# All norms of a fused two-layer transformer block: the variance and factor of a chunk taken in turn with the centering and square of the next

## The reference

```python
def _layernorm(x, axis=-1, eps=1e-05):
    m = jnp.mean(x, axis=axis, keepdims=True)
    v = jnp.var(x, axis=axis, keepdims=True)
    return (x - m) / jnp.sqrt(v + eps)

def rmsnorm(x, w):
    return x * jax.lax.rsqrt(jnp.mean(x * x, axis=-1, keepdims=True) + EPS) * w
...
x = L0_attn_a_x
x = x + _L0_attn_a_ref(_layernorm(x, axis=-1), ...)
x = x + _L0_ffn_ref(_layernorm(x, axis=-1), ...)
x = x + _L0_attn_b_ref(_layernorm(x, axis=-1), ...)
x = x + _L0_ffn_ref(_layernorm(x, axis=-1), ...)
x = x + _L1_attn_a_ref(_layernorm(x, axis=-1), ...)
x = x + _L1_ffn_ref(_layernorm(x, axis=-1), ...)
x = x + _L1_attn_b_ref(_layernorm(x, axis=-1), ...)
x = x + _L1_ffn_ref(_layernorm(x, axis=-1), ...)
```

## Time and profile before

| | |
|---|---|
| median of 3 runs | 1047.9 us (1047.13 to 1048.45) |
| profiled execution | 1043.13 us, span 1041.0 us |
| mean granted TensorE clock | 0.945 |
| PE busy | 949.4 us (91%) |
| ACT busy | 541.9 us (52%) |
| DVE busy | 535.3 us (51%) |
| POOL busy | 146.2 us (14%) |

### The profile page before, as it was taken

One profiled execution on the slowest core, in us unless ns is written; L12 is line 12 of the kernel. 1 busy time (PEld: TensorE's weight loads), 2 busy tenths in 40 slices (PEclk: granted clock), 3 DMA queues, 4 the chain that ended last, 5 costly groups with the idle time before them and its releaser, 6 DMA issues.

```text
span 1041.0 us, 23939 instructions
## 1 busy us (share of the span) xinstructions
PE 949.4 (91%) x10552; PEld 442.3 (42%) x10552; DVE 535.3 (51%) x870; ACT 541.9 (52%) x767; POOL 146.2 (14%) x164
## 2 busy tenths in 40 slices
PE   7489969899999988997899799997999999999998
PEld 4257743423333335883333334433333333344443
DVE  4356725733333266665465445546666666423554
ACT  6024445689999946443655551246454454445121
POOL 4101020331001003110011040000233223004000
PEclk9789999999999998559999899999999999998999
DMA  7653140010000000000000036400000000001651
GB/s 205 202 150 101 53 169 0 0 42 2 2 2 2 2 1 2 4 4 1 1 0 0 1 76 150 104 1 0 2 3 2 2 2 2 0 1 29 160 130 51
DMA packets 16479, 43.23 MB, mean 42 GB/s; under 512 B 4812, under 2 KB 5260, under 8 KB 14700
## 3 DMA queue, kind: packets, MB, share of 16 engines
q1 hardware_dynamic: 16376, 41.71, 14.7%
HBM read 36.91 MB, written 4.55 MB: 40 GB/s over the span
## 4 chain that ended last, share of the span: by engine, by line
PE 78%; ACT 8%; DVE 6%; issue 2%; DMA 2%; SPq 2%; POOL 1%; DVEq 0%; POOLq 0%
PE ps L1599 77%; ACT nrr L816 2%; ACT nrr L814 1%; DMA stf<-aux 1%; ACT work L1059 1%; POOL work L665 1%; SPq L578 1%; ACT work L860 0%; DVE mxq L1220 0%; DVE work L1553 0%; ACT nrr L803 0%; ACT nrr L800 0%; DVE stf L1567 0%; SPq L572 0%; DMA stf<-scr_k 0%
## 5 line engine op out<-in xcount | busy, mean ns | idle before, releaser
L1599 PE MATMUL ps<-rq,stf 32*64 32x512 f32 (+4 forms) x4096 | 213.5, 469 | 3.5 <-ACT hz L964 1.6
L1599 PE MATMUL ps<-work,vbuf 64*32 64x96 f32 (+6 forms) x3712 | 197.2, 386 | 2.4 <-issue 2.2
L1599 PE MATMUL ps<-hz,wsb 128*128 128x512 f32 (+1 forms) x352 | 159.3, 608 | 6.3 <-ACT nsq L805 3.5
L1599 PEld LDWEIGHTS ps<-rq,stf 32*64 32x64 f32 x4096 | 102.1, 152 | 108.4 <-issue 85.8
L920 ACT ACTIVATE work<-ps 128x1024 f32<-128x1024 f32 x144 | 139.4, 1022 | 13.4 <-PE ps L1599 10.0
L1599 PEld LDWEIGHTS ps<-work,vbuf 64*32 64x32 f32 (+1 forms) x3712 | 72.5, 121 | 112.6 <-issue 65.2
L982 ACT ACTIVATE work<-ps 128x1024 f32<-128x1024 f32 x72 | 73.6, 1024 | 75.7 <-PE ps L1599 75.7
L1599 PEld LDWEIGHTS ps<-hz,wsb 128*128 128x128 f32 (+1 forms) x352 | 61.7, 188 | 86.2 <-issue 67.5
L1301 DVE TENSOR_TENSOR work<-work,csb 128x1024 f32<-128x1024 f32 (+1 forms) x40 | 41.6, 1040 | 95.8 <-ACT work L920 95.4
L1028 ACT ACTIVATE work<-ps 128x512 f32<-128x512 f32 x48 | 28.7, 597 | 117.2 <-PE ps L1599 117.2
L1599 PE MATMUL ps<-work,wsb 128*128 128x512 f32 (+1 forms) x176 | 86.9, 602 | 2.7 <-DVE work L1514 2.7
(11 more groups left out here) (194 smaller groups left out, 1163.4 us busy)
## 6 DMA issues: line engine op xcount, KB each, us to landing
stf<-scr_w SPq DMA_DIRECT2D x32, 256.0 KB, 4.5
stf<-scr_w SPq DMA_DIRECT2D x64, 128.0 KB, 3.4
stf<-scr_k SPq DMA_DIRECT2D x12, 204.0 KB
stf<-scr_q SPq DMA_DIRECT2D x12, 192.0 KB
wsb<-in_w SPq DMA_DIRECT2D x1, 2192.0 KB, 11.0
rq<-in_rq SPq DMA_DIRECT2D x2, 1024.0 KB, 8.2
scr_q<-work SPq DMA_DIRECT2D x6, 256.0 KB, 5.1
scr_k<-work SPq DMA_DIRECT2D x6, 256.0 KB, 5.6
```

What stands on the lines that cost most here:

```text
L1599: return nc.tensor.matmul(o, l, r, start=start, stop=stop, skip_group_check=True)
```

## The change

TensorE takes center c + 1 ahead of mean c, and ScalarE square c + 1 ahead of factor c; before, each did one kind for all four chunks first. In the twins ScalarE runs two squares first. No instruction is added or dropped, and VectorE, GpSimd and SyncE keep their order.

```diff
             def norm(n):
                 src, _, kind, _, _, _ = nrm(n)
-                for c in range(NC):
+                e = eps[:, 0:1] if kind == "ln" else eps[:, 1:2]
+
+                def square(c):
                     if kind == "ln":
                         act.wait_ge(n_cen, centered_up_to(n, c))
                         nc.scalar.activation(nsq[:, c], bank(c), ACT.Square).then_inc(n_sq, 1)
...
+                def factor(c):
                     act.wait_ge(n_var, squared_up_to(n, c))
                     nc.scalar.activation(nrr[:, c], bank(4 + c), ACT.Ln, bias=e).then_inc(n_ln, 1)
-                    act.wait_ge(n_ln, i + 1)
+                    act.wait_ge(n_ln, 4 * n + c + 1)
                     nc.scalar.activation(nrr[:, c], nrr[:, c], ACT.Exp, scale=-0.5).then_inc(n_r, 1)
...
+                square(0)
+                if n not in TWINS:
+                    for c in range(1, NC):
+                        square(c)
+                        factor(c - 1)
+                    factor(NC - 1)
+                    return
+                square(1)
+                for c0 in range(0, NC, 2):
+                    for c in (c0, c0 + 1):
+                        twin_factor(c)
+                        if c + 2 < NC:
+                            square(c + 2)
+                    for c in (c0, c0 + 1):
+                        nc.scalar.activation(nsq[:, c], bank(4 + c), ACT.Ln, bias=eps[:, 0:1]).then_inc(n_ln, 1)
+                    if n != 2:
+                        for c in (c0, c0 + 1):
+                            hidden_factor(n, c)
...
             def norm(n):
                 src, _, kind, _, _, _ = nrm(n)
-                if kind == "ln":
-                    for c in range(NC):
+                for c in range(NC + 1):
+                    if c < NC and kind == "ln":
                         wait_source(pe, n, c)
                         mm(bank(c), c_("center"), ch(src, c)).then_inc(n_cen, 1)
-                for c in range(NC):
-                    pe.wait_ge(n_sq, squared_up_to(n, c))
-                    mm(bank(4 + c), c_("mean"), nsq[:, c]).then_inc(n_var, 1)
+                    if c:
+                        pe.wait_ge(n_sq, squared_up_to(n, c - 1))
+                        mm(bank(3 + c), c_("mean"), nsq[:, c - 1]).then_inc(n_var, 1)
```

More of the change, by code:

```diff
@@ L794, in norm @@
                         nc.scalar.activation(nsq[:, c], ch(src, c), ACT.Square).then_inc(n_sq, 1)
[L795 to L809, removed]
@@ L810, in norm, with twin_factor @@
-                e = eps[:, 0:1] if kind == "ln" else eps[:, 1:2]
-                for c in range(NC):
-                    i = 4 * n + c
+                def factor(c):
                     act.wait_ge(n_var, squared_up_to(n, c))
                     nc.scalar.activation(nrr[:, c], bank(4 + c), ACT.Ln, bias=e).then_inc(n_ln, 1)
-                    act.wait_ge(n_ln, i + 1)
+                    act.wait_ge(n_ln, 4 * n + c + 1)
                     nc.scalar.activation(nrr[:, c], nrr[:, c], ACT.Exp, scale=-0.5).then_inc(n_r, 1)
+                def twin_factor(c):
+                    _, e2, at = TWINS[n]
+                    act.wait_ge(n_var, squared_up_to(n, c))
+                    nc.scalar.activation(nrr[:, c], bank(4 + c), ACT.Ln, scale=1.0 + e2,
+                                         bias=eps[:, at:at + 1]).then_inc(n_ln, 1)
+                    act.wait_ge(n_ln, second(n, c))
+                    nc.scalar.activation(nrr[:, c], nrr[:, c], ACT.Exp, scale=-0.5).then_inc(n_r, 1)
```

## The result

The changed kernel took 1041.53 us in the median of 11 executions (1036.67 to 1048.25), the kernel before 1048.45 in 11 on the same chip (1041.99 to 1055.95): a ratio of 0.9941, 95% interval 0.9913 to 0.9968, or -6.2 us. The ratios are taken over the fast executions alone, the means that stand beside some of them over all, and the two ways differ by up to 2 us.

The account below looks back on a forecast made before the run. TensorE was taken to hold 78% of the chain of waits, ScalarE 8%. Norm by norm, -0.94 - 1.30 + 0.74 + 0.43 + 0.10 - 0.15 - 0.64 = -1.76 us, from 1047.9 to 1046.1 us, range 1043.2 to 1048.6.

Parts of the forecast that it names:

- The size of one norm: In a centered norm: first factor 1.7 us earlier, last factor 0.65 earlier, last variance matmul on TensorE ends 0.43 later.
- Norms 1 and 2: Norm 1, before a linear layer, gains 0.47 us; norm 2, a twin before VectorE's rotary product, gains 0.65.
- Norms 5 and 6: Norm 5, before a linear layer, gains 0.47 us; norm 6, before the location layer, where TensorE sets the pace, loses 0.43.
- Norm 4: No centering there; squares 2 and 3 now stand behind Exps, so last Exp and rotary product come later: loss 0.74 us.
- Norm 7: Before the router's gates, four groups of about 1 us that end about where they end now: gain 0.05 us.
- Norm 8: A twin, with VectorE as the chain to the residual that releases norm 10's centering: gain 0.65 us.
- Norm 12: Before the router's gates, four groups of about 1 us that end about where they end now: gain 0.10 us.
- all norms wait for the last factor: Rival: TensorE's queue never matters, so all eleven norms gain 0.65, 7.2 us together: 1040.8 us; chance 0.06.
- the low stretch behind norm 12 goes: Rival: the new order closes small gaps between the router's gates, ending the low clock, 2.9 us: 1043.2 us; chance 0.18.
- the fall behind norm 4: Rival: TensorE's new waits in norm 4 lower the clock through 15 us behind it, 7.5 us more: 1053.6; chance 0.07.
- table switches: Rival: squares between factors make ScalarE reload its activation tables in each norm: over 1100 us; chance 0.01.
- I carry the difference: Last step: median before lies 4.8 us above the profiled execution; this is kept, so 1047.9 - 1.8 = 1046.1 us.

Follow-up runs that it names:

- whole2: The changed kernel again, unaltered, on another chip, against the kernel before: ratio 0.9973 (0.9944 to 1.0001), -2.8 us.
- all_but_12: The changed kernel with the old order in norm 12 only, against the kernel before: ratio 1.0002 (0.9976 to 1.0028).
- null: The old order in every norm, written in the changed kernel's code (same program as before), against the kernel before: ratio 0.9981 (0.9951 to 1.0011).
- only_12: The kernel before with the new order in norm 12 only, against the kernel before: ratio 1.0006 (0.9978 to 1.0034).

## Why the prediction was wrong, and where it was right

The three comparisons of the changed kernel with the one before give -6.9, -1.8 and -1.8 us in the means (standard errors 1.7, 1.0 and 1.3), together -2.7 with 0.7. By the ratios they are -6.2, -2.8 and -0.2, together -3.3 with 0.9. The forecast of the change, -1.8, fits the second and third and the joint value; the first lies 2.4 of its errors from the mean of the three. What made that one -6.9 stays open: the clocks of its executions of the kernel before were not kept. No norm or group of norms gave by its total more than its step; the stage behind norm 12 did in the profiles.

- *The size of one norm.* The mechanism holds in every centered norm that was read: first factor earlier (-1.62, forecast -1.7), last factor -0.55 (forecast -0.65), TensorE's last mean later, +0.58 (forecast +0.43). The term that was missing is the 0.10 of a mean that waits for its square and has its weights loaded only then; it shifts all three the wrong way.
- *Norms 1 and 2:* -0.55 to z 3 and -0.50 from there, -1.05 in all; forecast -0.47 - 0.65 = -1.12.
- *Norms 5 and 6:* center to last z -0.56 or more (with the low clock at its start, 483 us, 9.43 before and 8.68 in whole3), then +0.72 to norm 6's last copy, the sum about +0.1; forecast -0.04.
- *Norm 4:* +0.74, as forecast, in every profile with the new order on both engines and full clock there (all_but_12 had a low stretch at 381, and 8.00 for 7.08).
- *Norm 7:* z 3 comes 0.5 to 0.6 earlier, and from there to the first routed share it takes 25.88 for 25.63 at full clock and 27.57 for 27.33 with a low stretch of 3.4 us: -0.3 in all; forecast -0.05.
- *Norm 8:* from the last residual ahead of it to its z 3 10.94 for 11.58, -0.64; forecast -0.65. *Norm 10:* +0.15; forecast +0.10. *Norm 11:* -0.56; forecast -0.64.
- *Norm 12:* z 3 -0.55, and 0.2 to 0.3 of it is left at the routed shares when profiles with an equal low stretch are compared; forecast -0.10. But in all three profiles of the changed kernel the low stretch was 3.4 us, and in both of the kernel before (before and null) 6.8, so the whole stage took 35.62 to 35.68 for 37.24 and 37.56: some 1.6 to 1.9 less. TensorE behind norm 12, before and then after:

```profile
936.54 3.19 PE L1599 MATMUL ps<-wsb,hz 128*128 128x16 f32 x16 [0.17 <-DVE hz L1122]
939.66 12.78 PE L1599 MATMUL ps<-hz,wsb 128*64 128x512 f32 x32
```

```profile
934.06 3.96 PE L1612 MATMUL ps<-wsb,hz 128*128 128x16 f32 x32
937.95 12.04 PE L1612 MATMUL ps<-hz,wsb 128*64 128x512 f32 x32
```

- *Norm 0:* no piece of it repeats well enough to say.
- Sum of the pieces at an equal low stretch: -1.7 to -1.9, against the forecast's -1.76. With the shorter stretch behind norm 12 it would be -3.2 to -3.5, which also fits the joint -2.7 and -3.3; the totals can't tell the two apart.

The rivals: that all norms wait for the last factor (1040.8) would have come nearest to the time, but for a wrong reason: norms 4, 6 and 10 lost as the steps say. The second, that the low stretch behind norm 12 goes, came by half: it was 3.4 us for 6.8 in every profile of the changed kernel. Its reason, the small gaps between norm 12's gates, is refuted by only_12 and all_but_12, which had it the other way round. In the profiles of the changed kernel the fall behind norm 4 didn't come, nor did table switches: the trace after has six loads, as before.

The step that failed is the last: "I carry the difference" from the profiled execution to the median, with a range of 1043.2 to 1048.6. It took the three shown runs, 1047.13 to 1048.45, as the spread of the kernel. It is 1036.4 to 1057.3 over 139 executions of it. The spread between executions had been put at nothing: the range adds up low stretches that I read in the one profile of before (2.9 us behind norm 12, 1.5 to 1.7 for one more), while most of the dozen places differ between executions of one kernel. A median of 11 against 11 with a deviation of 4 us has a standard error of about 2 by itself. The range should have been wider by that, some 1041 to 1050. That the first comparison came out at -6.2 is in part its draw of executions, since the two later ones lie nearer to the forecast, and in part open.

## What to carry to other kernels

When two engines hand one chunk after another to each other, lay out both queues as a recurrence with the measured durations before interleaving: here it gave the norm's own steps to within 0.2 us. What the stages behind them made of it was right to within 0.3 us at an equal clock. Interleave only where the source of the second engine's first step comes chunk by chunk (a center), not where it is there at once (norm 4), and change both queues or neither. Before believing a difference of 0.5%, run the same pair on another chip, and compare pieces of the program that repeat to 0.01 us rather than totals that don't.

## What was not expected of the hardware

- Identical instructions behind an identical wait were granted the higher or the lower clock from execution to execution (4.33 against 7.40 us at 886), with nothing in the kernel to tell them apart. From the start to norm 1 the changed kernel took 150.90, 154.71 and 156.44 us in its three profiles, at a mean granted clock of 0.94, 0.91 and 0.89.
- A pair of 128x512 records whose operand comes only when TensorE has reached it takes 1.12 to 1.13 us, against 1.02 in a full stream, even where no idle time stands in front of it (161.53). In a norm with the new order that hits the first mean and the last.
